# First cross-attention of a twelve-layer kernel: transposes by DMA instead of TensorE, a share of the rounding on GpSimd

## The reference

```python
q = (x @ Wq + bq); k, v = split(cond @ Wkv + bkv)       # x is layer-normed
q = _fq_sym(q / sqrt(16), axis=-1)                      # round to 127 levels, per row and head
k = _fq_sym(k, axis=-1)
v = _fq_sym(v, axis=2)                                  # one scale per column, over all 2048 rows
attn = softmax(q @ k.T)
attn = _fq_unsigned(attn, axis=-1)                      # round to 255 levels of the row's maximum
out = (attn @ v) @ Wp + bp
```

## Time and profile before

| | us |
|---|---|
| median of three runs (4005.96 to 4012.58) | 4011.17 |
| the profiled execution | 3993.2 |
| its span, first to last instruction | 3991.4 |

### The profile page before, as it was taken

How to read it: one execution, slowest core, us unless ns; L and a number is a source line. 1 busy time by engine, 2 the same in 40 slices (tenths; PEclk the granted TensorE clock), 3 DMA queues, 4 the chain that set the end, 5 groups by cost and what they waited for, 6 DMA issues and landing times. The chain is left out here.

```text
span 3991.4 us, 68700 instructions
## 1 busy us (share of the span) xinstructions
PE 3279.4 (82%) x26164; PEld 2316.7 (58%) x26166; DVE 2522.6 (63%) x5345; ACT 1700.4 (43%) x3261; POOL 423.8 (11%) x607
## 2 busy tenths in 40 slices
PE   7999998998877678773699695878899887877878
PEld 4555556887766355542365443535555555666767
DVE  6989987444346788887656473237777764444553
ACT  3889986111134535441244211225555542223232
POOL 3000000000000000000011003221121211111000
PEclk8556655999988667676799897989999998988787
DMA  2000001000001000001000104000000003000000
GB/s 86 1 0 0 0 0 50 30 0 0 21 11 34 23 2 2 2 2 65 6 8 5 51 20 127 21 3 4 5 3 3 3 3 129 1 0 0 1 1 11
DMA packets 45075, 73.25 MB, mean 18 GB/s; under 512 B 25821, under 2 KB 33505, under 8 KB 41189
## 3 DMA queue, kind: packets, MB, share of 16 engines
q1 hardware_dynamic: 36648, 70.28, 5.0%
q10 hardware_dynamic: 8256, 0.52, 0.2%
HBM read 67.65 MB, written 3.15 MB: 18 GB/s over the span
## 5 line engine op out<-in xcount | busy, mean ns | idle before, releaser
L1402 DVE TENSOR_SCALAR_CACHE_REDUCE l0x_ex<-l0x_s_ps 128x1024 f32<-128x1024 f32 x258 | 305.6, 1222 | 50.4 <-PE l0x_s_ps L1105 49.4
L1237 ACT ACTIVATE l0x_ex<-l0x_ex,l0x_neg_max,l0x_q_scale 128x2048 f32<-128x2048 f32 x128 | 268.0, 2093 | 51.2 <-DVE l0x_neg_max L1408 49.4
L1105 PE MATMUL l0x_s_ps<-l0x_kT,l0x_qT 64*128 64x512 bf16 x516 | 227.6, 580 | 35.3 <-ACT l0x_qT L1232 20.0
L1117 PEld LDWEIGHTS l0x_t_ps<-l0x_identb,l0x_pb 128*128 128x128 bf16 x2048 | 192.9, 139 | 109.6 <-issue 50.0
L1244 ACT ACTIVATE l0x_pt<-l0x_t_ps 128x1024 bf16<-128x1024 bf16 x256 | 246.1, 1013 | 20.5 <-PE l0x_t_ps L1117 20.2
L1117 PE MATMUL l0x_t_ps<-l0x_identb,l0x_pb 128*128 128x128 bf16 x2048 | 226.5, 297 | 10.2 <-ACT l0x_pt L1244 6.1
L1417 DVE TENSOR_SCALAR l0x_pb<-l0x_ex 128x2048 bf16<-128x2048 f32 x128 | 156.3, 1222 | 0.0
L263 PE MATMUL l3x_bank<-l3x_w_kv_x,l3x_ctxT 128*128 128x512 f32 x256 | 120.1, 612 | 26.6 <-ACT l3x_ctx_k L762 15.8
L1105 PEld LDWEIGHTS l0x_s_ps<-l0x_kT,l0x_qT 64*128 64x128 bf16 x516 | 48.4, 118 | 129.5 <-issue 74.1
L2198 PE MATMUL l1a_bank<-l1a_r,l1a_r 32*64 32x64 f32 x2048 | 78.6, 299 | 45.9 <-DVE l1a_r L2518 38.8
L2198 PEld LDWEIGHTS l1a_bank<-l1a_r,l1a_r 32*64 32x64 f32 x2048 | 73.0, 176 | 57.8 <-DVE l1a_r L2518 48.9
(11 more groups left out here) (746 smaller groups left out, 8140.6 us busy)
## 6 DMA issues: line engine op xcount, KB each, us to landing
l2f_wproj_raw<-in_L_xattn_wproj SPq DMA_DIRECT2D x2, 2048.0 KB, 12.4
l3a_w<-in_L_attn_W SPq DMA_DIRECT2D x4, 1024.0 KB, 11.5
l2f_w<-in_L_ffn_w SPq DMA_DIRECT2D x1, 2816.0 KB, 11.7
l0x_ctxT<-in_ctxT SPq DMA_DIRECT2D x8, 256.0 KB, 2.9
...
```

The source lines that it names most:

```text
L1105: ins = mm(s_ps[:, j * 512:(j + 1) * 512], qT[rows, h // 2, :], kT[rows, h // 2, j * 512:(j + 1) * 512], start=True, stop=True)
L1117: ins = nc.tensor.transpose(t_ps[:, j * P:(j + 1) * P], pb[:, h % 2, j * P:(j + 1) * P], identb[:])
L1237: s.activation(ex[:, h % 4, :], ex[:, h % 4, :], ACT.Exp, scale=q_scale[:, h:h + 1], bias=nb[:, h:h + 1], accum_out=sums[:, h:h + 1]).then ...
L1402: v.tensor_scalar(ex[:, h % 4, c], s_ps[:, c], 1.0, None, ALU.mult, ALU.max, accum_out=mx[:, h, half:half + 1]).then_inc(o.up(scores_taken ...
```

## The change

- SP loads the whole context first, eight transfers one behind the other, into `ex` (`ctxT` is now a view of two of its slots).
- TensorE makes all values first, in eight pieces of 512 columns over four banks (`values`), and then the eight key sets (`keys`, `turn_keys`). VectorE takes a piece's maximum when ScalarE has copied it. ScalarE does the first rounding pass of the values, VectorE the other two between the key sets 1 and 2, and rounds the first queries after set 3. Loops over pairs are unrolled.
- Values are transposed by two `dma_start_transpose` from SP instead of TensorE and ScalarE.
- Probabilities of each head are transposed by one `dma_start_transpose` from `pb` to `pt`, both now of four slots (`pt` lies over `vT`). SP waits for both roundings of the head, and for the mix of the head four before. `turn_probs` and `take_probs` are gone. `mix` runs four heads behind the scores.
- VectorE rounds columns 0 to 1023 of a head, in one instruction, GpSimd columns 1024 to 2047, in two (add, then subtract). VectorE's rounding stands between its two takings. The second taking starts from the first one's maximum.
- The two one-element instructions of the bias, and the copies of the query scales, move to ScalarE.
- `qT` is copied in two halves, the first after head 14, the second at head 0 of the next tile.
- Final clip and three-fold copy of the queries are one instruction instead of four.
- The output's transpose and projection use banks of `t_ps` instead of `misc`.
- The last tile stands outside the loop and prepares no next tile.

```diff
+        ctxT = ex[:, 0:DC, :]
+        pt = flat(vT[:]).bitcast(BF16).rearrange("p (u m) -> p u m", m=M)
+        DVE_PART, POOL_PART = slice(0, 1024), slice(1024, 2048)
...
+        def slot_turned(eng, t, h, before):
+            if h >= 4:
+                eng.wait_ge(turned[h % 4].sem, turned[h % 4].value(t, 16 * (h // 4)))
+            elif before:
+                eng.wait_ge(turned[h % 4].sem, turned[h % 4].value(t - 1))
...
+            for n in range(SETS):
+                sp.dma_start(ctxT[:, :, n * CH:(n + 1) * CH], d["ctxT"][:, n, :, :]).then_inc(ctx_loaded[n // 2].sem, 16)
             load_next(sp, env)
+            for m in range(DC):
+                sp.wait_ge(vi_ready.sem, vi_ready.value(0, m + 1))
+                sp.dma_start_transpose(vv[:, :, m * P:(m + 1) * P], vi[:, m, :]).then_inc(vv_turned.sem, 16)
+            for t in range(TILES):
+                for h in range(H):
+                    for rounded in (probs, pool_rounded):
+                        sp.wait_ge(rounded.sem, rounded.value(t, h + 1))
+                    if h >= 4:
+                        sp.wait_ge(mixed.sem, mixed.value(t, h - 3))
+                    elif t:
+                        sp.wait_ge(mixed.sem, mixed.value(t - 1, H + h - 3))
+                    sp.dma_start_transpose(pt[:, h % 4, :].rearrange("p (i q) -> p i q", q=P), pb[:, h % 4, :]).then_inc(turned[h % 4].sem, 16)
...
+            for n in range(PIECES):
+                values(n)
+            whole(norm.tensor(pe, 0, misc))
+            pe.wait_ge(parts_set.sem, parts_set.value())
+            for n in range(SETS):
+                keys(n)
+                if n == 2:
+                    queries(0)
+                if n >= 2:
+                    turn_keys(n - 2)
+                if n == 5:
+                    turn_queries(0)
...
-            def turn_probs(t, h, before):
...
             def mix(t, h, before):
+                pe.wait_ge(turned[h % 4].sem, turned[h % 4].value(t, 16 * (h // 4 + 1)))
                 for j in range(KT):
-                    ins = mm(o_ps[:, h * HD:(h + 1) * HD], pt[:, h % 2, j * P:(j + 1) * P], vv[:, j, h * HD:(h + 1) * HD], start=j == 0, stop=j == KT - 1)
+                    ins = mm(o_ps[:, h * HD:(h + 1) * HD], pt[:, h % 4, j * P:(j + 1) * P], vv[:, j, h * HD:(h + 1) * HD], start=j == 0, stop=j == KT - 1)
+                ins.then_inc(mixed.sem, 1)
...
             def exponentials(o, h):
-                act.wait_ge(max_ready.sem, max_ready.value(o.t, h + 1))
+                act.wait_ge(scores_taken.sem, scores_taken.value(o.t, 2 * h + 2))
+                s.activation(nb[:, h:h + 1], mx[:, h:h + 1], ACT.Copy, scale=q_neg[:, h:h + 1]).then_inc(o.up(), 1)
+                act.wait_ge(o.sem, o.at())
+                s.activation(nb[:, h:h + 1], nb[:, h:h + 1], ACT.Identity, bias=ln255[:]).then_inc(o.up(), 1)
+                act.wait_ge(o.sem, o.at())
                 s.activation(ex[:, h % 4, :], ex[:, h % 4, :], ACT.Exp, scale=q_scale[:, h:h + 1], bias=nb[:, h:h + 1],
...
+            def round_probs(o, t, h, before):                       # GpSimd
+                pool.wait_ge(exped.sem, exped.value(t, h + 1))
+                pool.sem_inc(o.up(), 1)
+                part = ex[:, h % 4, POOL_PART]
+                g.tensor_scalar(part, part, 1.0, MAGIC, ALU.mult, ALU.add).then_inc(o.up(), 1)
+                pool.wait_ge(o.sem, o.at())
+                slot_turned(pool, t, h, before)
+                pool.sem_inc(o.up(), 1)
+                g.tensor_scalar(pb[:, h % 4, POOL_PART], part, 1.0, -MAGIC, ALU.mult, ALU.add).then_inc(o.up(pool_rounded), 1)
...
             def take_scores(o, t, h, before):                       # VectorE
+                for rounded in (probs, pool_rounded):
+                    if h >= 4:
+                        dve.wait_ge(rounded.sem, rounded.value(t, h - 3))
+                    elif before:
+                        dve.wait_ge(rounded.sem, rounded.value(t - 1, H + h - 3))
+                dve.wait_ge(scores_ps.sem, scores_ps.value(t, 2 * h + 1))
+                v.tensor_scalar(ex[:, h % 4, 0:1024], s_ps[:, 0:1024], 1.0, None, ALU.mult, ALU.max, accum_out=first_max[:, h:h + 1]).then_inc(o.up(scores_taken), 1)
+                yield
+                dve.wait_ge(scores_ps.sem, scores_ps.value(t, 2 * h + 2))
+                dve.wait_ge(scores_taken.sem, scores_taken.value(t, 2 * h + 1))
+                v.tensor_scalar(ex[:, h % 4, 1024:2048], s_ps[:, 1024:2048], 1.0, first_max[:, h:h + 1], ALU.mult, ALU.max, accum_out=mx[:, h:h + 1]).then_inc(o.up(scores_taken), 1)
 
             def round_probs(o, t, h, before):
                 dve.wait_ge(exped.sem, exped.value(t, h + 1))
+                slot_turned(dve, t, h, before)
+                v.tensor_scalar(pb[:, h % 4, DVE_PART], ex[:, h % 4, DVE_PART], MAGIC, -MAGIC, ALU.add, ALU.add).then_inc(o.up(probs), 1)
```

More of the change, by code:

```diff
@@ L1154, in tile_steps @@
-                    if before and i == 4:
+                    if i + 1 < H:
+                        score(t, i + 1)
+                    elif more:
+                        score(t + 1, 0)
+                    if i >= 4:
+                        mix(t, i - 4, before)
+                    elif before:
+                        mix(t - 1, H + i - 4, before)
+                    if before and i == 5:
                         turn_out(t - 1)
-                    if before and i == 6:
+                    if before and i == 7:
@@ L1157, in tile_steps @@
                         project_out(t - 1)
-                    if i == H // 2:
+                    if more and i == 7:
                         whole(norm.tensor(pe, t + 1, misc))
-                    if i == H // 2 + 2:
+                    if more and i == 9:
                         queries(t + 1)
-                    if i == H - 2:
+                    if more and i == 13:
                         turn_queries(t + 1)
-            whole(norm.tensor(pe, 0, misc))
-            queries(0)
-            for u in range(2):
-                pe.wait_ge(kT_taken[u].sem, kT_taken[u].value(TILES // 2 - 1))
@@ L1189, in _ @@
+            tile_steps(last, True, False)
+            for h in range(H - 4, H):
+                mix(last, h, True)
             turn_out(last)
@@ L1312, in _ @@
-            main_order = L.sem("pool_main_order")
-            with pool.Fori(1, TILES + 1) as t:
+            for n in range(SETS):
+                u = n % 2
+                part = lambda i: k_parts[u][:, :, i * HD:(i + 1) * HD]
+                pool.wait_ge(k_rounded.sem, k_rounded.value(0, n + 1))
+                if n >= 2:
+                    pool.wait_ge(kT_ps.sem, kT_ps.value(0, 2 * (n - 1)))
+                pool.sem_inc(first.up(), 1)
+                g.tensor_copy(part(0), k_num[u][:]).then_inc(first.up(), 1)
+                pool.wait_ge(first.sem, first.at())
+                g.tensor_tensor(k_rest[:], k_num[u][:], part(0), ALU.subtract).then_inc(first.up(), 1)
+                pool.wait_ge(first.sem, first.at())
+                pool.sem_inc(first.up(), 1)
+                g.tensor_copy(part(1), k_rest[:]).then_inc(first.up(), 1)
+                pool.wait_ge(first.sem, first.at())
+                g.tensor_tensor(part(2), k_rest[:], part(1), ALU.subtract).then_inc(first.up(k_parts_ready), 1)
+                pool.wait_ge(k_parts_ready.sem, k_parts_ready.value(0, n + 1))
@@ L1314, in _, with tile_steps @@
+            def tile_steps(o, t, before, more):
+                for i in range(H):
+                    if more and i == 5:
+                        o.t = t + 1
+                        whole(norm.pool(o))
+                        o.t = t
+                    round_probs(o, t, i, before)
+            tile_steps(Order(pool, L.sem("pool_tile0_order")), 0, False, True)
+            with pool.Fori(1, TILES - 1) as t:
                 o = Order(pool, main_order, t - 1)
                 o.t = t
-                whole(norm.pool(o))
+                tile_steps(o, t, True, True)
```

430 lines of the change are left out of this document (171 added, 259 removed).

## The result

The changed kernel takes 3914.64 us (median of 4 runs, 3910.49 to 3920.03); the kernel before, run beside it, 4008.57 us (4001.07 to 4012.58). The ratio is 0.9767, with a 95% interval of 0.9744 to 0.9791: 94 us faster, where 103 were forecast (3908 us). The two profiled executions lie closer together, 3916.8 us of span against 3991.4, a gain of 74.6: the profiled run of before was itself faster than every timed one shown with it. What follows accounts for the 74.6.

The account below looks back on a forecast made before the run. TensorE and VectorE together were taken to bound the head at about 3.94 to 4.06 us. The stretch falls from 588.4 to 491 us (97), setting up by 6: -103 from the 4011.2 median gives 3908 us, own range 3870 to 3960.

Parts of the forecast that it names:

- TensorE and ScalarE relieved, the DMA hidden: Per head: TensorE left with 2.5 us, ScalarE with 2.8; a transposing DMA of 2 to 3.5 us costs nothing.
- The second rival: SP's queue: transposing DMA becomes the bound from 4.7 us per transpose; 4121 us at 5.5, 4428 at 7.9; chance 0.23.
- GpSimd's pass of 1.1 us: Each of GpSimd's two rounding passes over 128x1024 f32 takes 1.1 us, by the cast; ends 1.04 and 2.12.
- The third rival: GpSimd's rounding pass costs 2.12 us like the subtraction, 5.0 us per head: 4057 us; chance 0.08.
- the 1.5 us beside it: GpSimd's rounding pass at d = 1.5 us gives P = 3.9: +51 on the forecast, 3959 us.
- The lock: In rounding, VectorE's f32 SBUF pass waits until GpSimd's instruction is over, making a head 3.5 us, not 3.0.
- P = 2.4 + d: Steady head's pitch P, d being one GpSimd rounding pass: 3.5 us with d = 1.1.
- the first rival: VectorE's half slips between GpSimd's two passes, P is 3.0 us per head: 3841 us in all; chance 0.15.
- its objection: Against the interleaved order of 3.0 us: the first disturbance at a tile's end can drop it into the longer order.
- The part of a tile outside the heads: Per tile: VectorE's own part 4.4 us, plus 1.4 for its small instructions meeting GpSimd's, beside 56.0 of heads.
- The waits at the tile's end go: Waits at each tile's end vanish, since the queries' copy is in two halves and the first is read long before.
- Setting up, -6: Before the first taking: values first, their rounding between the key sets; -6 us booked, ends 0 and -12.5.

Follow-up runs that it names:

- e10: The changed kernel with GpSimd's half of the rounding left out, its columns set to zero once: 3883.65 us, 0.9675 of the kernel before.
- e6: The changed kernel with GpSimd's two rounding passes over its 1024 columns made one with two additions: 3903.33 us, 0.9742 of the kernel before.
- e5: The changed kernel with TensorE's query and output projections each given out in three pieces over three heads: 3894.53 us, 0.9715 of the kernel before.

## Why the prediction was right, and where it wasn't

**TensorE and ScalarE relieved, the DMA hidden: right.** 2 to 3.5 us were taken for a transposition; it costs 2.76 of the engines and lands in a median of 4.3 us (the page's row, `l0x_vT<-l0x_pb SPq DMA_TRANSPOSE x128, 4.3`). The second rival needed 4.7 us per head. The Trainium skill ("VectorE: DVE Perf Modes", section "The three transpose paths") gives 1309 ns for one block, sixteen one after another being an estimated 21 us per head; this case shows 2.76 for sixteen. ScalarE's small instructions were taken at 0.25, they take 0.29: ScalarE's head is 2.09 + 0.19 + 2 x 0.29 = 2.87 us, just under VectorE's.

**GpSimd's pass of 1.1 us: right**, 1.047 when free. The third rival, and the 1.5 us beside it, are out.

**The lock: right as a fact, wrong as a pace.** e10 shows that GpSimd's passes hold up VectorE's: without them every half takes 689 ns. The Trainium skill ("SBUF — State Buffer", section "SBUF: two separate sides") has the lock held for the whole instruction; the passes of 1.05 and 7.08 us agree, and e6's of 3.63 don't, since VectorE ran freely beside their middle. The Trainium skill ("SBUF — State Buffer", section "Who interferes with whom") also says that an instruction with at most one SBUF input, outside the two-port forms, stays clear of the lock, and the traces agree: VectorE's first takings from PSUM stay at 1221 ns and the reciprocal beside a 7 us pass took 0.25, where the `tensor_scalar` next to it took 6.74. But P = 2.4 + d assumed that VectorE's half always comes after GpSimd's second pass. It slips between the two, and the steady head is 2.95 us, not 3.5: 16 x 0.55 x 8 = 70 us too many. That was the first rival's order, and its objection was right as well: every disturbance in a tile drops some heads into collisions.

**The part of a tile outside the heads: too small.** 4.4 + 1.4 = 5.8 us were booked. A tile takes 510.7 / 8 = 63.8 us, 16 x 2.95 = 47.2 of it heads, so 16.6 are outside: 10.8 x 8 = 86 us too few. By the rows: the 4.4 booked, 3.4 us of collisions of the halves, 2.9 of the small instructions (1.4 booked), 4.2 of waits for scores and 0.7 for the output's product (none booked); one microsecond of the 16.6 is left open. The two errors cancel in the greater part: 491 forecast, 510.7 measured.

**The waits at the tile's end go: this step failed.** The half copies of the queries did most of what was said (0.5 and 0.4 us are left at a tile's end, where the earlier trace rows has 2.40), but the 44.3 us of waits in the tiles became 33.3, the longest of them now behind TensorE's projections, which stand in its queue ahead of the scores. I had booked none. A part of the earlier trace rows's 49.4, the 5.15 of the first scores, was never a wait between tiles. Projections stood in that queue before as well; with a head of 2.95 against TensorE's 2.5 a delay of some 3 us takes, by this difference, several heads to catch up. e5, which cuts them in pieces, brings the 33.3 down to 18.7.

**Setting up, -6: failed, +1.8.** The value products now run alone first, and the key loop's first reduction starts at 31.09 us instead of 20.26. I let half of the values' rounding hide in the key loop, but VectorE has no room there: it is busy without a pause from 31.1 to 72.9, and where GpSimd's work on the parts meets a pass of VectorE's, that one takes up to 0.8 us longer (1.26 instead of 0.43). Then 9.0 us pass from VectorE's last instruction on the keys, at 77.86, to the first taking:

```profile
81.41 1.15 POOL L1309 TENSOR_TENSOR l0x_k_parts<-l0x_k_rest,l0x_k_parts 128x512 bf16<-128x512 f32 x1
...
82.62 1.89 PE L1097 MATMUL l0x_t_ps<-l0x_identb,l0x_k_parts 128*128 128x128 bf16 x16 [3.80 <-POOL l0x_k_parts L1309]
83.70 1.94 ACT L1205 ACTIVATE l0x_kT<-l0x_t_ps 128x1024 bf16<-128x1024 bf16 x2 [3.75 <-PE l0x_t_ps L1097]
...
86.89 1.23 DVE L1415 TENSOR_SCALAR_CACHE_REDUCE l0x_ex<-l0x_s_ps 128x1024 f32<-128x1024 f32 x1 [8.34 <-PE l0x_s_ps L1140]
```

These are the rows of the kernel after: parts on GpSimd, transposes, copy, scores, each waiting for the one before. I had counted the passes taken off and not the serial start that was put in front. No experiment undid this part alone, so its account is read from the rows and not shown by a run.

**The total.** Taken from the profiles the gain is 74.6 us, and my 103 lay 28 above it: 19.7 from the tiles, 7.8 from setting up, 2.6 from the tail, less 1.3 in the other layers and rounding. Against the medians the error is only 7 us, because the profiled run of before was a quick one (15.4 us below its median) and that of after a slow one by 4. The parts that the gain rests on held: the transposes off TensorE, the DMA below the pace of VectorE, GpSimd's pass at its price. The pace of a head and the price of a tile did not, and that the number came so near is luck: two errors of 70 and 86 us that cancelled, and the choice of the median to subtract from. Of the prediction's signs, GpSimd's pass, VectorE's pass (0.69 free, 1.56 at most) and the landings came as said; the takings every 3.5 us, the first taking at 79 and the layer's end at 581 did not (2.95, 86.9, 610.5).
